# A two-layer graph network on one core: the neighbour values of groups 0 to 3 move into the rows of the first layer

## What is computed

```python
def L0(h, adj, W):
    Wh = h @ W.T
    norms = norm(Wh, axis=1)
    sim = Wh @ Wh.T / (norms * norms.T + EPS)
    alpha = softmax(where((adj > 0) | eye, sim, -inf), axis=1)
    return alpha @ Wh

def L1(x, adj, W_self, b_self, W_nb, b_nb, W_comb, b_comb):
    mask = adj > 0
    agg = mask @ x / max(sum(mask, axis=1), 1)
    combined = concat([x @ W_self + b_self, agg @ W_nb + b_nb])
    return relu(combined @ W_comb + b_comb)

x1  = layernorm(x + L0(x, adj, W))
out = layernorm(x1 + L1(x1, adj, ...))
```

## Time and profile before

| what | before |
|---|---|
| median of three runs | 919.47 us (919.01 to 919.75) |
| the profiled execution's own time | 918.97 us |
| its span (first to last instruction) | 917.2 us |
| TensorE busy | 882.7 us, 96% |
| VectorE busy | 610.8 us, 67% |
| ScalarE busy | 391.4 us, 43% |
| first layer, to the last attention matmul | ends at 630.0 |
| join, to the second layer's steady part | 630 to 700 |

### The profile page before, as it was taken

One profiled execution on the slowest core, in us unless ns is written; L12 is line 12 of the kernel. 1 busy time (PEld: TensorE's weight loads), 2 busy tenths in 40 slices (PEclk: granted clock), 3 DMA queues, 4 the chain that ended last, 5 costly groups with the idle time before them and its releaser, 6 DMA issues.

```text
span 917.2 us, 20896 instructions
## 1 busy us (share of the span) xinstructions
PE 882.7 (96%) x7151; PEld 711.8 (78%) x7151; DVE 610.8 (67%) x1302; ACT 391.4 (43%) x661; POOL 65.2 (7%) x175
## 2 busy tenths in 40 slices
PE   7989999999999999999999999998699999999997
PEld 6867777777777777777777777767488888888886
DVE  3787787888767887688778878998625333333333
ACT  4955655656656566556655656553210000000000
POOL 2300000000000000000000000011001100000000
PEclk9999999999999999999999999999799999999999
DMA  9235555565555655585567578742961323202200
GB/s 250 85 93 162 152 145 161 133 190 148 146 166 141 200 143 154 165 201 146 148 175 205 156 193 268 187 129 66 232 111 41 109 100 110 109 26 103 110 19 18
DMA packets 143213, 128.29 MB, mean 140 GB/s; under 512 B 64225, under 2 KB 120834, under 8 KB 142114
## 3 DMA queue, kind: packets, MB, share of 16 engines
q1 hardware_dynamic: 143058, 127.20, 48.6%
q0 software_dynamic: 80, 0.13, 0.1%
HBM read 95.83 MB, written 25.18 MB: 132 GB/s over the span
## 4 chain that ended last, share of the span: by engine, by line
issue 88%; POOL 5%; PE 4%; DMA 1%; DVE 1%; POOLq 1%; ACT 0%; SPq 0%; DVEq 0%
POOL rstd L523 3%; PE ps L1052 2%; POOL var_eps L521 1%; DMA feat<-xT 1%; PE ps L1064 1%; PE ps L1107 0%; POOLq L522 0%; PE ps L1134 0%; DVE work L685 0%; POOLq L520 0%; DVE work L797 0%; ACT prob_hi L589 0%; DVE big L677 0%; DVE mix_extremes L754 0%; POOLq L525 0%
## 5 line engine op out<-in xcount | busy, mean ns | idle before, releaser
L1156 PE MATMUL ps<-feat,prob_hi 128*128 128x257 f16 (+1 forms) x1024 | 279.9, 273 | 0.5
L1158 PE MATMUL ps<-feat,prob_lo 128*128 128x257 f16 (+1 forms) x1024 | 279.5, 273 | 0.0
L1157 PE MATMUL ps<-feat,prob_hi 128*128 128x256 f16 (+1 forms) x1024 | 278.9, 272 | 0.0
L1289 PE MATMUL ps<-big,mgroup 128*128 128x257 f16 x1024 | 226.2, 273 | 0.0
L1290 PE MATMUL ps<-big,mgroup 128*128 128x256 f16 x1024 | 226.2, 273 | 0.0
L829 DVE SCALAR_TENSOR_TENSOR prob_lo<-work,prob_hi 128x512 f16<-128x512 f32 x256 | 176.0, 687 | 75.2 <-ACT prob_hi L589 72.7
L589 ACT ACTIVATE prob_hi<-work 128x512 f16<-128x512 f32 x256 | 155.0, 626 | 102.5 <-DVE work L822 48.6
L582 ACT ACTIVATE work<-ps 128x512 f32<-128x512 f32 (+2 forms) x144 | 79.5, 557 | 130.8 <-PE ps L1086 113.4
L594 ACT ACTIVATE mask<-work 128x1024 fp8e4<-128x1024 f32 x128 | 133.8, 1045 | 0.0
L1157 PEld LDWEIGHTS ps<-feat,prob_hi 128*128 128x128 f16 x1024 | 100.3, 98 | 25.2
L1156 PEld LDWEIGHTS ps<-feat,prob_hi 128*128 128x128 f16 x1024 | 100.0, 98 | 25.5 <-DVE prob_lo L829 1.5
(11 more groups left out here) (120 smaller groups left out, 818.0 us busy)
## 6 DMA issues: line engine op xcount, KB each, us to landing
adj_sb<-adjT SPq DMA_DIRECT2D x128, 512.0 KB, 3.8
mask_spill<-mask SPq DMA_DIRECT2D x128, 128.0 KB, 2.7
mgroup<-mask_spill SPq DMA_DIRECT2D x8, 2048.0 KB, 8.2
xres<-x SPq DMA_DIRECT2D x8, 512.0 KB, 5.0
x1h_dram<-big SPq DMA_DIRECT2D x16, 256.0 KB, 5.2
out<-rows SPq DMA_DIRECT2D x32, 128.0 KB, 1.7
feat<-xT SPq DMA_DIRECT2D x7, 512.0 KB, 5.4
norm_bc<-norm_row_dram SPq DMA_DIRECT2D x8, 256.0 KB, 4.6
```

The costliest lines, as they stand in the source:

```text
L1156: pe.matmul(acc(D + 1), prob_hi[:, s, cols], feat_hi_of(g)[:, r, 0:D + 1], start=start, stop=False)
L1157: pe.matmul(acc(D), prob_hi[:, s, cols], feat_lo_of(g)[:, r, :], start=False, stop=False)
L1158: return pe.matmul(acc(D + 1), prob_lo[:, s, cols], feat_hi_of(g)[:, r, 0:D + 1], start=False, stop=stop)
L1289: pe.matmul(agg_ps(q, D + 1), lhsT, z_hi_of(g)[:, r, 0:D + 1], start=(jb == 0), stop=False)
```

## The change

- `values(0)` to `values(3)` run on TensorE in rows 3 to 6, after the diagonal and ahead of the first pair, into banks 2 and 3. ScalarE takes the heads at tile 0 of that pair and VectorE the tails at tile 1, and `attend_turned` waits for them before it writes these banks.
- SP loads x1 of groups 4 and 5 as soon as all scores are computed, ahead of x for group 7; the store and load of group 6 follow later, and the order behind that stays.
- In the join `values(4)` to `values(7)` use banks 2 and 3, 0 and 1, 4 and 5, 6 and 7; the neighbour sums use banks 2, 3, 0, 1 in place of 4 to 7, and the own products 4 and 5 in place of 0 and 1. So the first neighbour sums wait for the tails of group 4, and the wait for the attention's copies moves to `values(6)`.
- VectorE's `value_tails(4)` and `(5)` stand among group 6's pieces, where those of groups 0, 1 and 2 stood; none stand among group 7's any more. ScalarE does `value_heads(4)` and `(5)` right behind the first head of group 6.

```diff
-            return ps[:, 2 * (1 - slot) + half, :]
+            return ps[:, {5: 0, 6: 4, 7: 6}.get(g, 2) + half, :]
...
-            return ps[:, b % 2, 0:D]
+            return ps[:, 4 + b % 2, 0:D]
...
-            return ps[:, 4 + q, 0:width]
+            return ps[:, (2 + q) % 4, 0:width]
...
+                if a == G - 1:
+                    sync.wait_ge(score_done, G * NB)
+                    for g in range(EARLY, G - 2):
+                        load_x1T(g)
                 wait(sync, summed_ready, a * GB)
                 sync.dma_start(xres[:, :, :], x_v[a]).then_inc(xres_loaded, 16)
-                if a:
+                if 0 < a < G - 1:
                     store_x1(a - 1)
...
-            sync.wait_ge(score_done, G * NB)
-            for g in range(EARLY, G - 1):
-                load_x1T(g)
+            store_x1(G - 2)
+            load_x1T(G - 2)
             load_x1T(0)
...
                     heads(tile(j), j % GB)
+                    if j == 0 and group is not None:
+                        value_heads(group)
...
-            for q in range(GB):
-                x1_head(G - 2, q)
-                value_heads(q)
+            x1_head(G - 2, 0)
             value_heads(G - 4)
             value_heads(G - 3)
+            for q in range(1, GB):
+                x1_head(G - 2, q)
...
                     if j:
                         tails(tile(j - 1), (j - 1) % GB)
+                    if j == 1 and first and 0 <= a - 3 < EARLY:
+                        value_tails(a - 3)
...
-                    if a == G - 1 and n in (5, 9, 13):
-                        value_tails((n - 5) // 4)
+                    if a == G - 1 and n in (5, 9):
+                        value_tails(EARLY + (n - 5) // 4)
...
-            value_tails(3)
-            for n, piece in enumerate(between):
+            for piece in between:
                 piece()
-                if n in (0, 2):
-                    value_tails(4 + n // 2)
...
                 if qp == 0:
                     wait(pe, turned_copied, copied)
+                    wait(pe, z_ready, 2 * min(a - 2, EARLY))
...
             for a in range(G):
                 diagonal(a)
+                if 0 <= a - 3 < EARLY:
+                    if a == 3:
+                        pe.wait_ge(mixw_ready, 2)
+                    values(a - 3)
...
-            for g in range(G - 2):
+            for g in range(EARLY, G - 2):
                 values(g)
             pe.wait_ge(x1_ones_ready, G - 1)
-            pe.wait_ge(attn_copied, NB)
             pe.wait_ge(mgroup_loaded[0], 16)
+            pe.wait_ge(z_ready, 2 * (EARLY + 1))
```

More of the change, by code:

```diff
@@ L225, in attn_ps, with z_ps @@
             return ps[:, 4 + q, 0:width]
-        def z_ps(slot, half):
-            return ps[:, 2 * (1 - slot) + half, :]
+        def z_ps(g, half):
+            return ps[:, {5: 0, 6: 4, 7: 6}.get(g, 2) + half, :]
         def own_ps(b):
-            return ps[:, b % 2, 0:D]
+            return ps[:, 4 + b % 2, 0:D]
         def agg_ps(q, width):
-            return ps[:, 4 + q, 0:width]
+            return ps[:, (2 + q) % 4, 0:width]
         def x1T_of(g, h):
@@ L595, in unit_mask, with value_heads @@
                                saturate=False).then_inc(mask_ready, 1)
+            def value_heads(g):
+                for u in range(2):
+                    act.wait_ge(z_done, 2 * g + u + 1)
+                    act.activation(z_hi_of(g)[:, 2 * u:2 * u + 2, 0:D], z_ps(g, u).rearrange("p (b d) -> p b d", b=2),
+                                   ACT.Copy, scale=VALUE_SCALE).then_inc(z_hi_ready, 1)
             def diagonal(a):
@@ L608, in diagonal, with pair @@
                         unit_mask(u % 4, j - 1, 16 * (u // 4))
-            def pair(a, b):
+            def pair(a, b, group=None):
                 t0, f0, u0 = (first + more for first, more in zip(tiles_before(a), (GB, GB, 2)))
@@ L634, in _ @@
                     pair(0, 1)
+                early = a - 3 if 0 <= a - 3 < EARLY else None
                 if a < G - 2:
-                    with act.Fori(max(a + 1, 2), G - 1) as b:
-                        pair(a, b)
-                if a < G - 1:
[L639 to L647, removed]
+                    if early is not None:
+                        pair(a, a + 1, early)
+                    first = a + 2 if early is not None else max(a + 1, 2)
+                    if first < G - 1:
+                        with act.Fori(first, G - 1) as b:
+                            pair(a, b)
+                if a < G - 1:
+                    pair(a, G - 1, early if a == G - 2 else None)
             def x1_head(a, q):
@@ L889, in split_x1, with value_tails @@
                                          in1=x1_hi_of(a)[:, q, :], op0=ALU.mult, op1=ALU.subtract).then_inc(x1_ready, 1)
+            def value_tails(g):
+                for u in range(2):
+                    dve.wait_ge(z_hi_ready, 2 * g + u + 1)
+                    dve.scalar_tensor_tensor(out=z_lo_of(g)[:, 2 * u:2 * u + 2, :], in0=z_ps(g, u).rearrange("p (b d) -> p b d", b=2),
+                                             scalar=VALUE_SCALE, in1=z_hi_of(g)[:, 2 * u:2 * u + 2, 0:D],
+                                             op0=ALU.mult, op1=ALU.subtract).then_inc(z_ready, 1)
             def norm_work(a):
@@ L951, in pair @@
                 tails(tile(STEP_TILES - 1), GB - 1)
[L953 to L959, removed]
             between = []
@@ L1234, in pair @@
                         attend_turned(a, t, j % GB, qp, n * 4 + 2 * (halves + h))
[L1236 to L1250, removed]
             def combined(to, hi, lo, part, done):
@@ L1268, in values @@
                     hi, lo = x1T_of(g, 0), x1T_of(g, 1)
-                wait(pe, z_ready, 2 * (g - 1))
+                if g < EARLY:
+                    pe.wait_ge(turned_copied, 4 * sum(G - 1 - k for k in range(g + 3)))
+                if 0 < g <= EARLY:
+                    pe.wait_ge(z_ready, 2 * g)
+                if g == G - 2:
+                    pe.wait_ge(attn_copied, NB)
                 for b in range(GB):
                     cols = slice(b * P, (b + 1) * P)
-                    combined(z_ps(g % 2, b // 2)[:, (b % 2) * D:(b % 2 + 1) * D], hi[:, :, cols], lo[:, :, cols], 1,
+                    combined(z_ps(g, b // 2)[:, (b % 2) * D:(b % 2 + 1) * D], hi[:, :, cols], lo[:, :, cols], 1,
                              z_done if b % 2 else None)
+            front(0, None, 2)
+            for a in range(G):
+                diagonal(a)
+                if 0 <= a - 3 < EARLY:
+                    if a == 3:
+                        pe.wait_ge(mixw_ready, 2)
+                    values(a - 3)
+                if a == 0:
+                    pair(0, 1, False)
+                if a < G - 2:
+                    with pe.Fori(max(a + 1, 2), G - 1) as b:
+                        pair(a, b, False)
+                if a < G - 1:
+                    pair(a, G - 1, True)
+            pe.wait_ge(prob_ready, G * NB)
+            pe.wait_ge(turned_copied, G * (G - 1) * 2)
+            pe.wait_ge(mixw_ready, 2)
             def own(b):
@@ L1278, in own @@
                 pe.wait_ge(x1T_loaded[g], 16 * 2)
+                if b == 0:
+                    pe.wait_ge(z_ready, 2 * (G - 1))
                 wait(pe, own_ready, b - 1)
@@ L1292, in add_neighbours @@
                     ins.then_inc(agg_done, 1)
-            for g in range(G - 2):
+            for g in range(EARLY, G - 2):
                 values(g)
             pe.wait_ge(x1_ones_ready, G - 1)
-            pe.wait_ge(attn_copied, NB)
             pe.wait_ge(mgroup_loaded[0], 16)
+            pe.wait_ge(z_ready, 2 * (EARLY + 1))
             for b in range(GB):
                 for g in range(G - 2):
-                    if b == 0:
+                    if b == 0 and g > EARLY:
                         pe.wait_ge(z_ready, 2 * (g + 1))
```

## The result

| | before | after |
|---|---|---|
| median | 919.24 us (4 runs, 918.46 to 919.75) | 932.79 us (4 runs, 931.48 to 933.86) |
| ratio of after to before | | 1.0145, 95% interval 1.013 to 1.016 |
| span of the profiled execution | 917.2 | 932.0 |
| attention ends | 629.98 | 645.54 |
| from the end of attention to the end of `values(7)` | 55.8 | 54.9 |

A forecast was written before the change was run, and what follows sets the result against it. TensorE was taken to bound the first layer, and SP's queue of loads the join's end. Rows lose 13.9 us, the join gives 2.1: 11.8 slower, 918.97 becoming 930.8, plus 0.5 for the median, 931.3 us; range 926.0 to 935.5.

The forecast's parts named there:

- The reading of the bound: First layer: TensorE sets the pace, busy 567.7 of 578 us, so an added matmul costs its own time except in pauses.
- The rows, 13.9 us: First layer, rows 3 to 6: rows 3 to 5 lose 3.65 us each, row 6 loses 2.92; 13.9 us in all.
- The chain from last value matmul to the mask of tile 2: Rows 3 to 6: tile 4's scores wait for VectorE's tails, then tile 2's mask; 1.03 us of row 3's 3.65.
- The loads of groups 4 and 5: Start of the join: x1 lands at 634.2 and 636.9; the 9.08 us hole becomes a 4.2 us pause before `values(4)`.
- The clock behind that pause: Join, `values(4)` and `(5)`: clock stays full behind the 4.2 us pause, so nothing was added for it.
- the main case (40%): Whole kernel: the working as summed, clock full behind the 4.2 us pause; 11.8 us slower, 931.3 us.
- rival 1 (18%): Clock falls in the join's 4.2 us pause; the first 24 matmuls take 2.6 us more; 933.9 us, 18%.
- If the 4 us pause is followed by half clock: Join, behind the pause ahead of `values(4)`: one of three listed signs that the prediction is wrong.
- The queue and the new hole: Late join: SP stores group 7 at 669.4, its load lands at 678.5; TensorE stands 15 us, then `values(7)` takes 5.2.
- The join, 2.1 us gained: Join: `values(7)` ends at 683.7 instead of 685.77, a gain of 2.1 us.
- The total: Whole kernel: 13.9 us lost in the first layer, 2.1 gained in the join; 11.8 us slower, median 931.3 us.

The follow-up runs named there:

- Tails later: Changed kernel with VectorE's value tails in rows 3 to 6 moved one tile later, behind the mask of tile 2: 929.33 us, ratio 1.0104 to the kernel before.
- The filled pause: Changed kernel with 34 matmuls that nobody reads put into TensorE's 3.7 us pause ahead of `values(4)`: 930.43 us, ratio 1.0124 to the kernel before.
- Group 7 stored first: Changed kernel with SP's store and load of group 7 moved ahead of the loads of groups 1 to 3: 925.64 us, ratio 1.0075 to the kernel before.
- The rows alone: Changed kernel without early loads; heads and tails of groups 4 and 5 where they stood before: 928.32 us, ratio 1.0096 to the kernel before.
- tails behind: Changed kernel with heads and tails of groups 4 and 5 moved directly behind group 6's pieces: 926.34 us, ratio 1.0084 to the kernel before.
- all three: Changed kernel with tails one tile later, heads and tails of groups 4 and 5 behind group 6's pieces, and group 7 stored first: 912.31 us, ratio 0.9933.
- early loads: Kernel before with only SP's early loads of groups 4 and 5; values of groups 0 to 3 stay in the join: 915.41 us, ratio 0.9956.

## Why the prediction was right, point by point

- **The reading of the bound.** Right. TensorE sets the pace of the first layer: with the tails out of the way, rows 3 to 5 cost the 2.62 us of their matmuls each. Only the pause ahead of row 6's turned scores took some of the work in, 0.7 us, as forecast.
- **The rows, 13.9 us.** Measured 15.0. The chain from last value matmul to the mask of tile 2 was right to 0.15 us in all four rows: 3.79, 3.79 and 3.67 for 3.65, and 2.96 for 2.92. The rest is 0.4 ahead of `values(1)` and 0.3 between rows 5 and 6, which the working did not have. Tails later showed that the wait was VectorE's order, by 3.5 us in time and 4.0 in the rows.
- **The loads of groups 4 and 5.** Right: from attention's end to `values(4)` it is 3.9 us, printed as a pause of 3.73, for 4.2.
- **The clock behind that pause.** Wrong in the main case (40%), which left it full: it halved, as rival 1 (18%) had it. "If the 4 us pause is followed by half clock" stood among the prediction's own signs of being wrong, and it came. The filled pause showed both the cause and the price, 1.7 us on the values and 2.4 to 2.6 in the whole. This is the term that was mis-sized: put at nothing, it cost 1.7, and group 6 was stored 17.2 us behind attention's end where I had 15.8. The rival's 2.6 us was the price of all 24 matmuls at half clock; here the clock was back after the first 18. The total lies between the two cases, 932.8 against 931.3 and 933.9.
- **The queue and the new hole.** Right: `values(7)` began 49.8 us behind attention's end for 48.5, after 15.19 us of printed pause for 15.3, at half clock. Group 7 stored first showed that SP's order set it. Two misses in it nearly cancel: from the issue of the masks to the store of group 7 it took 15.5 us for 14.46, and `values(7)` started 4.7 us behind the issue of its load, for 5.5.
- **The join, 2.1 us gained.** Measured 0.9, mostly by the clock. Here something was missing from the working. I counted the store of group 6 against before, where three pairs of tails stood among the pieces, and found it 0.6 late; I did not see that with those tails gone from there it could have been 5.6 us early, and that the tails of groups 4 and 5 in that place took this and more. The working priced what leaves the join, not where the rest stands in it. The rows alone, whose time I missed by 6 us, brought it out, and tails behind showed it.
- **The total.** 13.6 us for 11.8 by the medians, 14.8 by the profiled executions: 1.1 more in the rows, 1.2 less gained in the join, and the 0.6 that the two traces stand apart ahead of row 3.

What stays open is why 0.4 us are lost ahead of `values(1)` and 0.3 between rows 5 and 6; they stand in every trace that has the values in the rows.

## What to carry to other kernels

Work moved out of a pause is worth only what the next arrival behind it allows: before moving it, follow the last input of the stage (here store and load of group 7) back through its queue, and reorder that first; two edits to a DMA queue's order gave 8.6 us where the change as a whole cost 13.6. An instruction that waits for another engine goes behind whatever in the same in-order queue a third engine is waiting for: one tile later for the tails in the rows was worth 3.5 us, and eleven and seven pieces later for the tails of groups 4 and 5 in the join, with ScalarE's heads, 6.5. An engine that already sets the pace of a stage has no free place for work there but its own pauses.

## What the runs showed of the hardware

TensorE's clock fell in pauses that I had taken for short. Behind pauses of 3.56 to 3.73 us, in five traces (the changed kernel, tails one tile later, tails behind, group 7 stored first, all three), the next 48 matmuls took 6.9 to 8.1 us instead of 5.2; behind one of 3.10 us, the next 24 took 4.15 instead of 2.62. Behind the pause of 1.69 us at the start of row 7 the clock was full. A pause filled with matmuls that nobody reads kept it full, and was worth some 2.4 us here.

The same instructions do not always meet the same clock. From 51 to 54 us all twelve kernels do the same work on TensorE, behind pauses of 1.4 and 0.8 us. In four traces (tails later, early loads, rows only, pause filled) the granted clock was 0.50 to 0.55 there, in the other eight 1.00. It cost those four 1.0 to 1.3 us up to row 3. No run shows what decides it. A single execution's time should not be read closer than that.

The transposes behind the 2 MB load were held up: in all eight traces that have them there, the issue of the second one took 5.9 to 8.0 us against 1.3 elsewhere. It ended within 0.2 us of the landing of the 2 MB, which came 8.0 to 10.2 us after its own issue. In the changed kernel with group 7 stored first, a store issued 4.5 us behind the same 2 MB was held up too, 6.3 us from store to load in place of 3.7; issued 6.7 to 8.1 us behind it (three traces), it took 3.1.
